# A hand-pipelined attention layer on one core: the order of a step's work changed on all five engines

## The reference

```
q = heads(norm(x2) @ Wq)                        # 16 heads of 64
sim = (q @ k_text.T + q . rel_k[dist]) / 8      # 77 text columns, dist = clip(j - i, -16, 16) + 16
attn = softmax(sim)
out = attn @ v_text + sum_j attn[i, j] * rel_v[dist[i, j]]
out += softmax(q @ k_img.T / 8) @ v_img * (tanh(alpha) + 1)     # 16 columns
out += softmax(q @ k_aud.T / 8) @ v_aud * (tanh(beta) + 1)      # 35 columns
x3 = x2 + out @ Wo + bo
```

## Time and profile before

| | |
|---|---|
| median of 3 runs | 1164.21 us (1162.24 to 1169.32) |
| the profiled execution, own time | 1165.82 us |
| its span | 1164.0 us |
| TensorE busy | 1009.1 us, 87% |
| VectorE (DVE) busy | 665.6 us, 57% |
| ScalarE (ACT) busy | 406.5 us, 35% |
| GpSimd (POOL) busy | 386.7 us, 33% |
| mean granted TensorE clock | 0.961 |

### The profile page before, as it was taken

The page is one execution under the profiler, slowest core; times in us unless marked ns, Lnnn a source line. Parts: engine busy times, 40 slices in busy tenths (PEclk is TensorE's granted clock), DMA queues, the critical chain, the costliest instruction groups (busy, mean ns, idle before and its releaser), DMA issues. The chain is left out here.

```text
span 1164.0 us, 23711 instructions
## 1 busy us (share of the span) xinstructions
PE 1009.1 (87%) x7428; PEld 792.3 (68%) x7429; DVE 665.6 (57%) x1607; ACT 406.5 (35%) x877; POOL 386.7 (33%) x481
## 2 busy tenths in 40 slices
PE   4888888845899999979997999999998985899996
PEld 4676666743466666647365888888887964888885
DVE  2788877764233333321105777677676572699994
ACT  2554444421222222213332445444453441222221
POOL 1243333431122222235001554644544432133332
PEclk9999999967999999989999999999999987899998
DMA  4444444334811111136673679888887752011110
GB/s 120 126 141 141 137 138 133 128 122 160 293 45 45 45 42 48 45 96 233 239 241 112 167 212 224 200 229 211 209 226 187 175 142 49 28 42 41 41 32 28
DMA packets 193657, 153.41 MB, mean 132 GB/s; under 512 B 130368, under 2 KB 176960, under 8 KB 193472
## 3 DMA queue, kind: packets, MB, share of 16 engines
q1 hardware_dynamic: 173568, 93.70, 30.6%
q10 hardware_dynamic: 16960, 50.58, 11.7%
q0 software_dynamic: 3072, 8.39, 2.3%
HBM read 84.80 MB, written 67.83 MB: 131 GB/s over the span
## 5 line engine op out<-in xcount | busy, mean ns | idle before, releaser
L1462 POOL TENSOR_TENSOR c_soft<-c_soft,c_share 128x616 f32<-128x616 f32 (+2 forms) x96 | 71.7, 774 | 136.5 <-DVE c_share L1890 134.6
L968 POOL TENSOR_TENSOR b_up<-b_up,b_gate 128x512 f32<-128x512 f32 x39 | 49.4, 1267 | 189.0 <-DVE b_up L1095 189.0
L2176 PE MATMUL d_CV<-d_hp,ffn_tap 128*128 128x128 f32 x768 | 95.3, 282 | 3.8 <-DVE d_hp L2253 3.4
L2176 PEld LDWEIGHTS d_CV<-d_hp,ffn_tap 128*128 128x128 f32 x768 | 90.9, 197 | 7.9 <-DVE d_hp L2253 5.1
L494 PE MATMUL a_M<-early 128*128 128x128 f32 x512 | 73.3, 289 | 9.3 <-ACT early L411 9.3
L1029 PE MATMUL b_G<-moe_w,b_rowsT 128*128 x156 | 76.0, 610 | 3.1 <-ACT b_rowsT L977 2.7
L1060 PEld LDWEIGHTS b_Y<-moe_w,b_hidT 128*128 128x128 f32 x312 | 59.3, 190 | 25.1 <-issue 19.2
L1060 PE MATMUL b_Y<-moe_w,b_hidT 128*128 x312 | 73.8, 380 | 0.8 <-ACT b_hidT L993 0.8
L494 PEld LDWEIGHTS a_M<-early 128*128 128x128 f32 x512 | 63.4, 196 | 16.0 <-ACT early L411 7.5
L1029 PE MATMUL b_U<-moe_w,b_rowsT 128*128 x156 | 73.4, 593 | 0.0
L1092 DVE TENSOR_TENSOR b_gate<-b_G,moe_b 128x512 f32<-128x512 f32 x39 | 27.0, 692 | 71.1 <-PE b_G L1029 70.3
(11 more groups left out here) (234 smaller groups left out, 2286.6 us busy)
## 6 DMA issues: line engine op xcount, KB each, us to landing
rel_windows<-c_relw ACTq DMA_DIRECT2D x32, 816.0 KB, 6.3
c_bias<-rel_windows SPq DMA_DIRECT2D x16, 616.0 KB, 4.9
prob_rows<-c_soft SPq DMA_DIRECT2D x16, 616.0 KB, 5.4
moe_w<-in_L_Wl SPq DMA_DIRECT2D x16, 512.0 KB, 3.8
values<-c_soft ACTq DMA_DIRECT2D x15, 512.0 KB, 3.4
b_rows<-expert_lists SPq DMA_DIRECT2D x39, 128.0 KB, 2.1
expert_out<-b_out SPq DMA_DIRECT2D x39, 128.0 KB, 1.7
c_v<-values SPq DMA_DIRECT2D x16, 308.0 KB
```

The lines of the kernel that those rows point to most:

```text
L968: nc.gpsimd.tensor_tensor(up[p][:, :], up[p][:, :], gate[p][:, :], ALU.mult).then_inc(g["hid"], 1)
L1462: ins = nc.gpsimd.tensor_tensor(soft[p][:, hs, a:z], soft[p][:, hs, a:z], share[:, s, hs].unsqueeze(2).to_broadcast([P, HS, z - a]), ALU.mult)
L2176: ins = nc.tensor.matmul(CV[:, m, :], tap[:, m, k, :], hp[p][:, m, k:k + P], start=(k == 0), stop=(k == 2))
```

## The change

TensorE's step becomes: scores half 0, **rows(b + 2)**, probabilities 0 and 1, scores half 1, weighted 0 to 2 with probabilities 2 and 3 between, then a piece of ready work (even step: the first half of the queries; odd step: the first pair of key tiles), weighted 3, the rest of the keys, the rest of the queries, distances, and last **bands(b - 1) and output(b - 1)**. ScalarE follows with the same order, exps half 0 after the four probs, exps half 1 between the attended halves.

DVE's step becomes: choice of rows of b + 4, less_max of both halves, shares half 0, ends(b - 1), shares half 1, rows(b + 3), rows_normal(b + 3), output(b - 1). Rows are therefore made one batch earlier; rows of batch 2 are made before the loop. rows now also writes x2 + bo into x2b, which has a place for each of the 16 batches, so residual leaves GpSimd and nothing waits for it. The folded term is added to the first three places of x2b and to bo before the loop. GpSimd's step becomes: gather(b + 4), normalise of both halves, inverse_std(b + 3), tails(b). far loses its first 16 columns for each head (they were multiplied by zero).

relw keeps only the 92 columns that change. The 112 zero columns are written to both rel_windows once before the loop, from a tile of zeros; windows then writes 92 columns for each head, 368 bytes in one run. SP issues rel_in before the store and band_in.

```
             def steps(b, i, p, first, last):        # TensorE
                 turns.begin(b, i, p)
+                ahead = there(b + 2)
                 scores(b, i, p, 0)
+                if ahead:
+                    n_rows = rows(b + 2, p)
...
+                def ready_work():
+                    if p == 1 and ahead:
+                        context(i + 1)
+                        projected(wk[0], PAIR_TILES[:1])
+                    elif ahead:
+                        query(n_rows, 0)
...
+                if p == 1 and ahead:
+                    projected(wk[0], PAIR_TILES[1:])
+                    query(n_rows, 0)
+                if ahead:
+                    query(n_rows, 1)
+                    distances(p)
                 if not first:
-                    n_probs = [probabilities(b - 1, 1 - p, 0), probabilities(b - 1, 1 - p, 1)]
-                scores(b, i, p, 1)
-                if not first:
-                    attend(b - 1, i - 1 + p, 1 - p, n_probs)
-                if p == 1 and there(b + 2):
-                    context(i + 1)
-                    projected(wk[0])
-                if not first:
-                    n_bands = bands(b - 1, i - 1 + p, 1 - p)
-                if there(b + 2):
-                    n_rows = rows(b + 2, p)
-                if not first:
-                    output(b - 1, n_bands)
-                if there(b + 2):
-                    queries(n_rows)
-                    distances(p)
+                    output(b - 1, bands(b - 1, i - 1 + p, 1 - p))
...
             def steps(b, i, p, first, last):        # DVE
-                if there(b + 3):
-                    pick_rows(b + 3, i + 1 + p, 1 - p)
-                if there(b + 2):
-                    rows(b + 2, i + 1, p)
+                if there(b + 4):
+                    pick_rows(b + 4, i + 2, p)
+                less_max(b, i, p, 0)
+                less_max(b, i, p, 1)
+                shares(b, p, 0)
                 if not first:
                     ends(b - 1, 1 - p)
-                less_max(b, i, p, 0)
-                if there(b + 2):
-                    rows_normal(b + 2, p)
-                less_max(b, i, p, 1)
-                for h in range(2):
-                    shares(b, p, h)
+                shares(b, p, 1)
+                if there(b + 3):
+                    rows(b + 3, i + 1 + p, 1 - p)
+                    rows_normal(b + 3, 1 - p)
                 if not first:
                     output(b - 1, i - 1 + p, 1 - p)
...
+            sp.wait_ge(s_clear, 1)                  # SP, before the loop
+            for p in two:
+                sp.dma_start(rel_d[p][:, :, 0:REL_LO + 1], zeros[:, :].unsqueeze(1).to_broadcast([P, NH, REL_LO + 1])).then_inc(s_blank, 16)
...
-                    act.dma_start(rel_d[p][:, h * HS:(h + 1) * HS, :], w[:, :, :]).then_inc(s_relout[h], 16)
+                    act.dma_start(rel_d[p][:, h * HS:(h + 1) * HS, REL_LO + 1:RELW], w[:, :, :]).then_inc(s_relout[h], 16)
```

More of the change, by code:

```diff
@@ L1230, in attention1 @@
         x2 = [sb(f"c_x2{p}", [P, D]) for p in two]
-        x2b = [sb(f"c_x2b{p}", [P, D]) for p in two]
+        x2b = sb("c_x2b", [P, NB, D])
         x3 = [sb(f"c_x3{p}", [P, D]) for p in two]
@@ L1242, in attention1 @@
         v = [sb(f"c_v{p}", [P, INNER]) for p in two]
-        relw = [sb(f"c_relw{h}", [P, HS, RELW]) for h in two]
+        relw = [sb(f"c_relw{h}", [P, HS, RELW - REL_LO - 1]) for h in two]
+        zeros = sb("c_zeros", [P, REL_LO + 1])
         bias = [sb(f"c_bias{p}", [P, NH, TEXT]) for p in two]
@@ L1300, in attention1 @@
         s_x3 = [sem(f"c_x3out{p}") for p in two]
-        names = "filled emptied pick x2 var rstd xn x2b s_mm s_sub s_exp share soft tails bandv pv_mm o_sb y_mm x3"
+        names = "filled emptied pick x2 x2b var rstd xn s_mm s_sub s_exp share soft tails bandv pv_mm o_sb y_mm x3"
         g = {n: sem("c_" + n) for n in names.split()}
@@ L1480, in _ @@
             inverse_std(1, 1)
+            gather(3, 1)
+            inverse_std(2, 0)
             pool.wait_ge(s_w, W_READY)
@@ L1601, in _ @@
                 act.wait_ge(out, 16 * (MT1 // 2))
-            def behind(b):
-                for k in range(4):
-                    probs(k)
-                attended(b)
             def steps(b, i, p, first, last):
                 turns.begin(b, i, p)
+                ahead = there(b + 2)
+                if ahead:
+                    rows()
                 if not first:
-                    behind(b - 1)
-                if p == 1 and there(b + 2):
-                    projected(kT, PAIR_TILES[:2])
-                    exps(b, p, 0)
-                    projected(kT, PAIR_TILES[2:])
-                    exps(b, p, 1)
+                    for k in range(4):
+                        probs(k)
+                exps(b, p, 0)
+                if p == 1 and ahead:
+                    projected(kT, PAIR_TILES[:1])
+                if not first:
+                    attended(b - 1, 0)
+                if p == 1 and ahead:
+                    projected(kT, PAIR_TILES[1:2])
+                if p == 0 and ahead:
+                    query(p, 0)
+                exps(b, p, 1)
+                if p == 1 and ahead:
+                    projected(kT, PAIR_TILES[2:3])
+                if not first:
+                    attended(b - 1, 1)
+                if p == 1 and ahead:
+                    projected(kT, PAIR_TILES[3:])
+                    query(p, 0)
+                if ahead:
+                    query(p, 1)
+                    windows(b + 2, i + 1, p)
                 if not first:
                     bands()
-                if there(b + 2):
-                    rows()
-                if p == 0 or not there(b + 2):
-                    for h in two:
-                        exps(b, p, h)
-                if there(b + 2):
-                    queries(p)
-                    windows(b + 2, i + 1, p)
             by_batch(steps)(act)
-            behind(NB - 1)
+            for k in range(4):
+                probs(k)
+            for h in two:
+                attended(NB - 1, h)
             bands()
@@ L1691, in queries, with query @@
             def queries(n_rows):
+                for u in two:
+                    query(n_rows, u)
+            def query(n_rows, u):
                 taken(n_rows)
-                for u in two:
-                    n, bank = turn()
-                    for j in range(MS):
-                        m = u * MS + j
-                        for c in range(KD):
-                            ins = nc.tensor.matmul(bank[:, j * P:(j + 1) * P], wq[:, c, m * P:(m + 1) * P], xT[:, c, :],
-                                                   start=(c == 0), stop=(c == KD - 1))
-                    ins.then_inc(g["filled"], 1)
+                n, bank = turn()
+                for j in range(MS):
+                    m = u * MS + j
+                    for c in range(KD):
+                        ins = nc.tensor.matmul(bank[:, j * P:(j + 1) * P], wq[:, c, m * P:(m + 1) * P], xT[:, c, :],
+                                               start=(c == 0), stop=(c == KD - 1))
+                ins.then_inc(g["filled"], 1)
             def context(i):
@@ L1795, in steps, with nothing @@
+            def nothing():
+                pass
             def steps(b, i, p, first, last):
                 turns.begin(b, i, p)
+                ahead = there(b + 2)
                 scores(b, i, p, 0)
[L1798 to L1805 removed]
@@ L1920, in _ @@
             nc.vector.tensor_copy(first_v[:, :], relT["v"][:, 0:1].to_broadcast([P, P])).then_inc(s_steps, 1)
+            dve.wait_ge(g["filled"], FIRST_ROWS + 1)
+            rows_normal(2, 0)
             dve.wait_ge(s_ffn, 32)
```

126 lines of the change are left out of this document (72 added, 54 removed).

## The result

The changed kernel takes 1170.56 us (median of 14 runs, 1168.45 to 1174.02), the kernel before 1165.67 (14 runs, 1160.85 to 1170.48). The ratio is 1.0045, with a 95% interval of 1.003 to 1.006: slower by about half a per cent, where 1151 and a gain of over 1% was forecast. The profiled execution took 1170.31 us with a span of 1168.5 and a clock of 0.958, against 1165.82, 1164.0 and 0.961, so the two traces differ by as much as the runs do, and can be compared stage by stage.

What follows compares the result with a forecast made beforehand. TensorE, busy 87% of the span, was taken as the bound, its removable idle time mainly band waits. Gains 11.5 + 1.5 + 0.9 + 0 - 0.5 = 13.4 us took 1164.2 to 1151, range 1146 to 1162.

Steps and rivals of the forecast that it cites:

- Who is next late: Prediction's timing of the loop's engine queues: xn ready at 17.4 us, wanted by TensorE at 19.3, slack 1.9 us.
- the slower rival: Loop through xn 5.5 us longer than worked out, GpSimd slowed by DVE; even steps 21.8, time 1174; chance 0.08.
- the ready work: Every step: work ahead of the last weighted covers its wait for copied probabilities, gaining 0.17 us a step.
- the mechanism: Steps 2 to 13: new order removes TensorE's band wait; 11.5 us from even steps, 1.5 from odd ones.
- The wait for xn of batch 3: Beginning of step 1: TensorE idles some 4 us, plus about 1.2 for lower clock; step 2 still starts 0.9 earlier.
- Zeros: Before the loop: writing zeros beside the short keys' way out costs 0.5 us, bounds 0 and 3.
- The fold: Before the loop: adding the folded term to 3 x 256 columns on DVE starts first scores 0.6 us later.
- the code of step 12: Rival: step 12's wait is for its own instructions, so 3.6 us stay; 1154.5, chance 0.12.
- x2b's 39 us: Steady loop: DVE's wait for GpSimd's x2b, 39 us in ten batches; its removal was valued at nothing.
- transfers of short runs: Loop's windows: about 25 ns a run, share about 0.79, no gain or loss; rival at 50 ns: 1164, chance 0.05.
- ends' waits of 4 us in steps 14 and 15: Loop's end: with nothing ahead to do, TensorE waits 4 us for DVE's ends, now behind shares.
- the tail: Steps 14, 15 and drain: 50.5 us before, 49.7 to 51.5 after; gain 0, bounds -1 and +1.

## Why the prediction was wrong

**The step that failed** is in "Who is next late": "DVE's rows_normal ends at 17.4 ... slack 1.9 us". Up to that point the sum was good. In the changed kernel, from the even step's start at 807.46, ends is over at 11.8 (11.6 worked out), shares of the second half at 13.75 (13.7), soft at 16.2 (16.1). The sum then lets inverse_std follow soft at once, which needs rows to be over by then, and takes rows_normal at 0.4. But the two multiply-adds of rows, 0.48 us each elsewhere, take 2.4 beside normalise, so GpSimd waits 1.19 us for DVE's variance (c_agg), and rows_normal takes 2.36 beside tails: xn at 20.8, 3.4 us later than worked out, against a slack of 1.9. TensorE, itself 0.7 us late by then, waits 0.93. I had these durations from places where GpSimd was not multiplying, and asked in the slower rival only whether GpSimd is slowed by DVE. It was the other way round: normalise takes 2.20 + 2.38 us, no more than the 4.7 allowed for, and DVE stood. That rival had the right loop, with 1.5 us over the slack where it reckoned 3.6; its chance of 0.08 was too small for a loop that closes with under 2 us of slack. That its 1174 lies near the measured time is luck: the waits for xn are 4.5 us of the miss, and most of the rest is in terms that it took over unchanged.

**Boundaries.** Even steps were to take 18.2 and take 18.87; 18.76 with rows later. 0.17 of it is the ready work, which gives nothing. A third of a us is the two bank waits shown above: the eight transposes of probabilities take 810.05 - 808.83 = 1.22 us behind rows, and 820.30 - 819.28 = 1.02 behind the scores in the version with rows later, where that bank is not in their way; the distances take 820.56 - 818.54 = 2.02 us ahead of the bands, and 1.89 ahead of the scores in the kernel before. The prediction followed ScalarE's copies of probabilities and queries, but not of these two banks. The remaining 0.17 is spread over other changes from one group to the next, and no run singles it out. Odd steps were to take 22.6 and take 24.06 - 0.93 = 23.13 without their wait. Over six pairs these sizes are 0.67 x 6 + 0.53 x 6 = 7.2 us, of which the version with rows later still has 5.5 (250.3 against a forecast of 244.8). I had added the times of groups as if their order were free; on these terms the mechanism was right and the sum too small.

**Step 1.** The wait for xn of batch 3 was foreseen, at 4 us and with 1.2 for the clock; it is 5.14, with another 2.38 ahead of it for ScalarE's query copy, and steps 0 and 1 take 42.8 instead of 39.0. The xn here has its 2.35 us beside tails as well, and the low clock lasts from the query wait on. Making batch 3's rows ahead too is worth 4.8 us in the medians.

**Zeros and fold.** Zeros were 0.5, within bounds of 0 and 3, and cost about 2 us in the short keys' stage: the cover, a double buffer, does not last. The fold, 0.6, measured 0.64: the first scores wait 1.21 us for DVE's c_wrel at 635.99, where they waited 0.57 for ScalarE before.

**What was right.** No band wait in steps 2 to 13; the code of step 12 was not its cause, for its wait went with the others; no gain of its own for x2b's 39 us (in the new order their going may be a condition, as the order alone suggests); transfers of short runs no bound (share 0.77), the loop the same either way; ends' waits of 4 us in steps 14 and 15 (4.33 and 4.34); the tail at 49.8 in bounds of 49.7 to 51.5.

The miss in sum, against the profiled execution: 1170.3 - 1152.4 = 17.9 us. Of it 11.7 lie in steps 2 to 13 (4.5 the five waits for xn, 7.2 boundaries and the ready work's missing gain), 6.9 ahead of step 2 (1.4 the unexplained start, some 2 the zeros, 3.8 steps 0 and 1, less the 0.5 charged), and -0.7 behind. Against the medians 1.5 us more are missed, since the forecast of 1151 starts from the first three runs of the kernel before, 1164.2, and fourteen give 1165.67.

## What to carry to other kernels

When work is moved, its duration has to be taken from a place with the same neighbour on the other engine: look for the longest instance of each group, not only its mean, and ask what ran beside it. When a wait is taken out by a new order, work out for every queue the time at which each result is ready and at which it is wanted, and spend the freedom that the new order gives on the smallest slack. Here moving two transposes 2 us later made +0.45% into -0.34%, and with the waits at both ends seen to, -1.35%. An order that loses alone (+2.5%) may be a part of the one that wins.

## What the runs showed of the hardware

- DVE stands until GpSimd's instruction ends: multiply-adds and a tensor_scalar over 128x256 take 0.48 and 0.41 us alone, 1.45 and 2.36 beside a GpSimd multiplication, 2.90 beside a longer one; a copy of 128x2 integers takes 0.16 alone and 1.74 beside it. Reductions keep their time (1.33 us for the three of shares).
- GpSimd pays much less: half a normalise takes 2.20 us and 2.38 beside the multiply-adds. In the kernel before tails takes 2.81 us at 817.00, and 3.02 at 837.56, where a DVE multiply-add had begun 0.14 us ahead of it.
- Writing a batch's windows in 2048 short runs (2 x 368 KB) or in 256 long ones (2 x 816 KB) made no difference to steps of 18.8 and 23.0 us.
- The zeros, 4096 runs of 448 bytes, lengthen the stage that they fall beside by about 2 us (24.7 to 26.7, or 36.7 to 38.5).
- Covering a wait on TensorE with a piece of other work gained nothing: 16 + 16 projections around a weighted product take 3.87 us and 32 in one piece 3.67, about the 0.17 us that was covered.
